# Two-layer decoder in one kernel: layer 1's attention in even rounds, transposes for selections, 23 expert slots

## The chip, the cores and the metric

The kernel runs on one core of a Trainium2 chip. The metric is device time in microseconds (us) of the whole kernel, median of several runs. TensorE, VectorE, ScalarE, GpSimd and SyncE are called PE, DVE, ACT, POOL and SP as in the profile; PEld is TensorE's loading of stationary operands.

## The reference, cut to what matters

The input is x, 8 sequences of 256 tokens by 128 features (2048 tokens, 16 tiles of 128), and a context of 8 x 256 x 256. All is float32. Six blocks follow each other, each added to x, each on a layer norm of x:

```python
x = x + _L0_attn_ref(_layernorm(x), ...)          # gated linear attention, 8 heads, chunks of 64
x = x + _L0_xattn_ref(ctx_2048, _layernorm(x), ...)   # attention over the context, 8 heads of 16
x = x + _L0_ffn_ref(_layernorm(x), ...)           # top 1 of 8 experts, silu(a) * g @ w2
x = x + _L1_attn_ref(_layernorm(x), ...)          # latent attention, 16 heads of 8 + 4 rotated, causal
x = x + _L1_xattn_ref(ctx_2048, _layernorm(x), ...)   # attention over the context, 8 heads of 16
x = x + _L1_ffn_ref(_layernorm(x), ...)           # top 1 of 8 experts, relu, b1, b2

# _L1_attn_ref, its core
Q = concat([Qc, rope(Qr)]); K = concat([Kc, rope(Kr)])      # 12 of 32 rows used per head
scores = clip(Q @ K.T, -80, 80); scores = where(causal, scores, -inf)
attn = softmax(scores / sqrt(12)) @ V; return attn @ W_O
# _L1_xattn_ref, its core
logits = (query * 16 ** -0.5) @ K.T + b[0] + -1e30 * (1 - mask); out = softmax(logits) @ V
```

## The kernel before, in words

The 16 tiles of tokens are worked on in four quads of four tiles, that is two sequences (batches) each. In time the kernel has five stages: layer 0's attention over all quads; the sort of tokens to expert slots; layer 0's experts, which write to the DRAM tensor x_mid; layer 1's attention (causal, then context); sort and experts again, which write the output. The change is almost wholly in the fourth stage.

Every engine's instructions are written by generators, one for each quad and part (`pe_mla` and `pe_xattn` for PE, `dve_mla`, `act_mla` and so on). Each generator yields the time at which its next piece should stand, and `alternate` merges the pieces of all generators by these numbers. So a table of numbers fixes the order of each engine's queue; what really starts when is decided by semaphores. In layer 1 a quad has the period `L1_PERIOD`, 72 planned units.

A head takes a strip of 32 rows of PE's array; four heads fill it. The work of a quad in layer 1:

- **In-work.** Layer norm, four transposes of tokens (`pe_ln`, L283, by way of the helper), the latent product (L1196), the rotated queries (L1199), four products for the keys (L1202, 512 columns each), values (L1207), and for each group g of four heads the queries in two accumulating products: the plain part (L1222) and `sel_rope`, which puts the rotated part `tq` in place (L1223).
- **Causal units.** 16 units of two heads and one batch. A unit is four score products (L1242, rows 32-strip by 256 or 128 columns) into one of two pairs of PSUM banks; then DVE clips and masks (L1398, 768 columns, writes `am`), ACT takes the exponential (L1340), and PE multiplies with the values, two units in one group (L1259), into bank 7; ACT copies that (L1328).
- **Out-work.** For each batch eight products with `m_sel` (L1268) sum up and turn to tokens, DVE divides, two transposes, two products with W_O, and DVE adds to x.
- **Context units.** They belong to the quad before. For each batch four units "M" (L826, scores, then DVE's maximum L1075 over 1024 columns), a turn of the maxima to rows ("N", L852, ACT copy, DMA into a row of the queries), four units "E" (L839, scores the other way round, ACT's exponential L1004), value products (L874), and "T", four products with `x_sel` to tokens (L884). Except in the last quad they all use one pair of PSUM banks (`use_bank` gives 2).
- **Router.** Layer norm, four transposes, logits (L970), `pe_rank`, and some 30 small DVE instructions that place the tokens.

A unit of two heads takes strips 0 and 1 or strips 2 and 3. `warm` (L278) issues products that nobody reads. In the trace a product shows as two records and a transpose as one, so "L826 x8" is one unit of four products.

The experts run in `TURNS = SLOTS // 4 = 6` turns of four slots of 128 rows: `hidden(s)` (L1538), `rows_out(s)` (L1548), DVE's sum (L1647), and POOL's indirect DMA (L1455).

Of the kernel before, what the change touches and what calls it, by code (L numbers as in the profile page):

```python
# [44 lines left out]
SLOTS = 24  # L45
COL_PROB, COL_ID, ROW = 2 * D, 2 * D + 1, 2 * D + 2
# [6 lines left out]
X_COLS, M_COLS = D + XH, D + MH  # L53
# [3 lines left out]
L0_PERIOD, L1_PERIOD = 57.0, 72.0  # L57
# [3 lines left out]
def alternate(*programs):  # L61

    waiting = [[next(p), k, p] for k, p in enumerate(programs)]
    while waiting:
        first = min(waiting, key=lambda w: w[:2])
        try:
# [9 lines left out]
              ("block_mask", 128), ("reset", 512), ("x_sel", XG * X_COLS), ("iota8", 8),  # L76
# [4 lines left out]
              ("clip_mask", 3 * 128), ("lat_rope", 256), ("q_rope", 256), ("m_sel", MG * M_COLS), ("sel_rope", MG * 128)]  # L81
# [3 lines left out]
               ("r0_w", EXP), ("r0_b", EXP), ("m_lat", 128), ("m_qr", 128), ("m_q", MG * 128),  # L85
# [17 lines left out]
def build(nc, A):  # L103
    ctx = ExitStack()
    with ctx:
# [48 lines left out]
        gla_own = sb("gla_own", [P, 2 * QN])  # L154
# [71 lines left out]
        kept = sb("kept", [P, 2, 4, 2 + D])  # L226

# [21 lines left out]
        def dve_ln_stats(v, s, n, q):  # L249
            for j in range(QT):  # L250
                v.bn_stats(stats[s][:, j, :], x_all[:, q * QT + j, :]).then_inc(S(s + "_stats"), 1)
            v.wait_ge(S(s + "_stats"), (n + 1) * QT)
# [1726 lines left out]
```

## Time and profile before

| what | us |
|---|---|
| median of 3 runs (880.88, 880.92, 897.6) | 880.92 |
| the profiled execution | 885.41 |
| its span, first to last instruction | 883.1 |
| layer 1's attention in it, x_mid in SBUF to layer 1's last logits | 364.8 (434.6 to 799.4) |
| PE busy, DVE busy, ACT busy | 714.6, 426.4, 265.8 |
| mean granted clock of PE | 0.894 |

The profiled execution lies 2.3 above its span and 4.5 above the median. Busy time of PE contains waiting inside the pipeline and grows when the clock is lower, so it says little alone.

### The profile page before, as it was taken

The page shows a single profiled execution, that of the slowest core. Times are in us where ns is not written, and L with a number is a line of the kernel's source. Part 1 is how long each engine was busy: PE and PEld are TensorE (multiplying, and loading weights), DVE is VectorE, ACT ScalarE, POOL GpSimd, SP SyncE. Part 2 cuts the span into 40 slices and gives each one's busy share as a digit, 9 for nine tenths or more (in the row PEclk, how much of TensorE's full clock was granted, in tenths as well). Part 3 has the DMA queues.
Part 4 walks back from the last instruction along what each step waited for, and adds up shares of the span by engine and source line. Part 5 has one row for each costly group of instructions (what it writes and reads, how often), then busy time and mean ns, then how long its engine had stood idle before and what let it go on. Part 6 is the DMA issues. An engine that isn't in the chain of part 4 may idle for free.

```text
span 883.1 us, 13749 instructions
## 1 busy us (share of the span) xinstructions
PE 714.6 (81%) x5218; PEld 475.4 (54%) x5219; DVE 426.4 (48%) x1130; ACT 265.8 (30%) x457; POOL 141.2 (16%) x163
## 2 busy tenths in 40 slices
PE   4788988888988863899698888898889888863885
PEld 2353554554555442899446455555464556432775
DVE  1556466756736425233245553555446644533453
ACT  1323323422430220222135135213522352130331
POOL 3221021211211102133200100100110011021333
PEclk9988999999998786999789997988699879885998
DMA  9600000000002004677310000100010001002762
GB/s 351 258 26 0 2 1 25 25 2 25 6 21 97 35 38 142 193 229 235 107 66 32 1 1 2 49 0 2 25 49 1 2 25 50 1 25 66 206 182 71
DMA packets 37798, 59.07 MB, mean 67 GB/s; under 512 B 9520, under 2 KB 26032, under 8 KB 36848
## 3 DMA queue, kind: packets, MB, share of 16 engines
q1 hardware_dynamic: 34384, 46.76, 17.1%
q0 software_dynamic: 3072, 7.38, 2.3%
q10 hardware_dynamic: 288, 4.19, 1.3%
q8 instruction: 36, 0.59, 0.3%
q14 instruction: 18, 0.15, 0.1%
HBM read 50.68 MB, written 13.71 MB: 73 GB/s over the span
## 4 chain that ended last, share of the span: by engine, by line
PE 67%; DVE 11%; ACT 9%; issue 5%; DMA 5%; POOL 2%; SPq 1%; POOLq 0%; ACTq 0%; DVEq 0%
PE ps L1538 7%; PE ps L826 7%; PE ps L278 6%; PE ps L839 6%; PE ps L874 4%; PE ps L1548 4%; PE ps L1242 3%; DVE neg_max L1075 3%; PE ps L1259 2%; ACT pT L1004 2%; PE ps L884 2%; PE ps L1222 2%; PE ps L1268 2%; PE ps L1202 2%; PE ps L896 2%
## 5 line engine op out<-in xcount | busy, mean ns | idle before, releaser
L1075 DVE TENSOR_REDUCE neg_max<-ps 128x4 f32<-128x1024 f32 x64 | 78.2, 1225 | 77.9 <-PE ps L826 77.8
L278 PE MATMUL ps<-cst 128*128 128x512 f32 (+1 forms) x126 | 74.5, 725 | 36.4 <-DMA sorted<-rows_all,pos 24.6
L1398 DVE SCALAR_TENSOR_TENSOR am<-ps,cst 128x768 f32<-128x768 f32 x64 | 60.2, 953 | 45.8 <-PE ps L1242 45.8
L1538 PE MATMUL ps<-pT,w 128*128 128x128 f32 x576 | 72.6, 280 | 10.7 <-issue 5.6
L1340 ACT ACTIVATE w<-am 128x768 f32<-128x768 f32 x64 | 53.9, 842 | 81.1 <-DVE am L1398 72.4
L1538 PEld LDWEIGHTS ps<-pT,w 128*128 128x128 f32 x576 | 67.9, 194 | 14.0 <-issue 10.0
L1440 POOL DMA_INDIRECT sorted<-rows_all,pos x32 | 32.7, 1021 | 189.4 <-DVE pos L393 182.1
L1242 PE MATMUL ps<-qa,ka 32*128 32x128 f32 (+1 forms) x512 | 61.3, 375 | 0.3 <-DVE am L1398 0.3
L278 PEld LDWEIGHTS ps<-cst 128*128 128x128 f32 x126 | 26.6, 233 | 64.3 <-issue 56.1
L1242 PEld LDWEIGHTS ps<-qa,ka 32*128 32x128 f32 x512 | 48.4, 208 | 15.7 <-issue 9.1
L839 PE MATMUL ps<-qs,gla_own 32*128 32x256 f32 x256 | 44.6, 493 | 10.0 <-ACT pT L1004 8.3
L826 PE MATMUL ps<-gla_own,qs 32*128 32x256 f32 x256 | 40.3, 436 | 12.1 <-ACT pT L1004 7.4
L1002 ACT ACTIVATE pT<-ps 128x1024 f32<-128x1024 f32 x32 | 32.4, 1024 | 54.6 <-PE ps L839 54.1
L1004 ACT ACTIVATE pT<-ps,wts 128x1024 f32<-128x1024 f32 x32 | 35.5, 1112 | 28.8 <-PE ps L839 28.7
L826 PE MATMUL ps<-ka,qs 32*128 32x256 f32 x256 | 33.7, 411 | 9.5 <-DVE qs L1059 5.0
L271 POOL TENSOR_TENSOR ve_x<-mv_x,cst 128x4 f32<-128x4 f32 x16 | 4.1, 254 | 231.2 <-DVE mv_x L255 231.2
L826 PEld LDWEIGHTS ps<-gla_own,qs 32*128 32x128 f32 x256 | 23.8, 200 | 26.7 <-DVE neg_max L1075 8.8
L839 PEld LDWEIGHTS ps<-qs,gla_own 32*128 32x128 f32 x256 | 27.3, 239 | 19.2 <-ACT pT L1004 11.8
L1091 DVE RECIPROCAL rden<-ps 128x16 f32<-128x16 f32 x16 | 4.1, 257 | 68.0 <-PE ps L884 68.0
L839 PE MATMUL ps<-qs,ka 32*128 32x256 f32 x256 | 34.1, 428 | 3.0 <-DMA qs<-nm_rows 2.7
L1259 PE MATMUL ps<-w,vm 128*32 128x128 f32 (+1 forms) x512 | 33.7, 379 | 1.7 <-ACT w L1328 0.5
L721 POOL TENSOR_TENSOR qe_bd<-gla_own,cst 128x512 f32<-128x512 f32 x16 | 17.0, 1073 | 105.9 <-DVE gla_own L633 58.1
(249 smaller groups left out, 1268.1 us busy)
## 6 DMA issues: line engine op xcount, KB each, us to landing
w<-in_w SPq DMA_DIRECT2D x24, 512.0 KB, 3.6
sorted<-in_no_rows SPq DMA_DIRECT2D x2, 3096.0 KB, 23.2
w<-in_w SPq DMA_DIRECT2D x24, 256.0 KB, 3.0
w<-in_w ACTq DMA_DIRECT2D x2, 2048.0 KB, 8.7
pT<-sorted SPq DMA_DIRECT2D x12, 256.0 KB
kept<-sorted SPq DMA_DIRECT2D x12, 256.0 KB
ctxT<-in_ctxT SPq DMA_DIRECT2D x4, 512.0 KB, 4.2
gla_own<-in_keys SPq DMA_DIRECT2D x4, 512.0 KB, 4.4
```

Source lines behind the costliest of these rows:

```text
L278: pe.matmul(bank(b)[:, 0:cols], ident, cst[:, 0:cols], start=True, stop=True)
L826: i = pe.matmul(bank(use_bank(layer, "M", e, q) + jj)[:, qt * T:(qt + 1) * T], qs[r, g, q0:q0 + P], kl[r, g, b * T:(b + 1) * T], start=Tru ...
L839: i = pe.matmul(bank(use_bank(layer, "E", e, q) + jj)[:, kt * T:(kt + 1) * T], kl[r, g, k0:k0 + P], qs[r, g, b * T:(b + 1) * T], start=Tru ...
L874: i = pe.matmul(bank(V_BANK[layer], STRIP, STRIP * k)[:, g * T:(g + 1) * T], xv[layer][:, 2 * b + kt, h0 + k, :], p, start=(kt == 0), stop ...
L1004: i = a.activation(out, scores, ACT.Exp, bias=W("x1_b"))
L1075: v.tensor_reduce(neg_max[:, 2 * b:2 * b + 2, h0:h0 + 2].rearrange("p t j -> p j t"), ps[:, p:p + 2, :].rearrange("p j (t k) -> p j t k", ...
L1242: i = pe.matmul(bank(M_PAIRS[u % 2][jj])[:, to], ka[r:r + STRIP, g, b * T + lo:b * T + lo + P], qa[r:r + STRIP, g, b * T + lo:(b + 1) * T] ...
L1259: i = pe.matmul(o, vm[:, 2 * b + kt, 2 * hp + k, :], p, start=(kt == 0), stop=(kt == 1), skip_group_check=True)
L1340: a.activation(view[0], view[1], ACT.Exp, scale=float(MD + MR) ** -0.5).then_inc(S("mp"), 1)
L1398: v.scalar_tensor_tensor(out[:, :, 0:3 * P], ps[:, 4 * (u % 2):4 * (u % 2) + 2, 0:3 * P], -CLIP, C("clip_mask").unsqueeze(1).broadcast_to( ...
L1538: k = pe.matmul(bank(lane(s) + 1 + half)[:, at * P:(at + 1) * P], w1[:, s * cols + c * P:s * cols + (c + 1) * P], xsT[:, s, :], start=True ...
L1548: k = pe.matmul(bank(lane(s))[:, 0:D], hidT[s][:, j * P:(j + 1) * P], wsrc[:, bass.ds(es[s] * (4 * D) + j * D, D)], start=(j == 0), stop=( ...
```

## The change

Layer 0's attention keeps its order; only its "T" step becomes four transposes with the identity instead of four products with `x_sel` (136 columns), and DVE picks the heads out of the strips. Layer 1's attention is rewritten:

- The unit of time is a **round**, one causal unit n = 0 to 63, over all four quads without a break. Context units stand at fixed rounds: for batch h M at 8h + 13, 14, 17, 18 and E ten rounds later, so from round 13 on a round has at most one. By these numbers the context unit takes strips 0 and 1 when the causal unit takes 2 and 3, and the other way round. It stands ahead of the causal unit on PE.
- From unit 12 on all causal units use the pair of banks 0 and 1 (`m_pair`), and the context units banks 2 and 3, until the causal ones are done; then they take turns on both pairs. All other work shares banks 4 and 5 in turn (`SHARED`, `wait_for_shared`).
- In-work of a quad is spread over rounds 4.7 to 16.6 of the quad before, out-work over the rounds after. Keys, values and some queries have a second buffer (`m_keys`, `m_values`, `qa_odd`).
- Queries: two products `m_qa` and `m_qb` of the latent, DVE multiplies by the rotation, multiplies the other half and adds (three instructions in place of one); then one product for each four heads in place of two.
- `m_sel` is gone: eight transposes for a batch instead of eight products of 144 columns; DVE divides tile by tile.
- Layer 1's context keys come in 8 pieces into three buffers, its values in 8 pieces.
- `keep_busy` puts a product that nobody reads (256 columns) ahead of each context unit after round 65.
- POOL sets `mask_row` (128 x 2048) to 1 after the first experts.
- 23 slots (`USED`) are worked instead of 24: the last turn of each expert stage has three.

The core of the diff:

```diff
+USED = B * T // P + EXP - 1
-L0_PERIOD, L1_PERIOD = 57.0, 72.0
+L0_PERIOD = 57.0
...
+        MU = MH // 2
+        MX = QB * MU
+        X_LAG = 13
+        def xm_at(h, i):
+            return MU * h + X_LAG + i // 2 * 4 + i % 2
+        def xe_at(h, i):
+            return MU * h + X_LAG + 10 + i // 2 * 4 + i % 2
+        IN_AT = {"ln": 4.70, "lat": 5.70, "qa": 6.20, "qb": 6.70, "k": (7.30, 7.70, 8.30, 14.10), "v": 10.80,
+                 "q": (13.60, 14.85, 15.20, 16.60)}
+        IN_AT_0 = dict(IN_AT, k=(7.20, 17.15, 17.60, 19.40), v=15.60, q=(7.70, 16.70, 17.90, 20.60))
+        OUT_AT = {"tok": (9.45, 9.70), "turn": 10.05, "out": 10.55, "strips": 11.40, "N": X_LAG + 7.85, "T": X_LAG + 18.60}
+        R_AT = {"L": X_LAG + 28.90, "R": X_LAG + 29.40, "rank": X_LAG + 31.40}
+        def shared(*use):
+            return 4 + SHARED.index(use) % 2
+        def m_pair(n):
+            return 2 if n < X_LAG - 1 and n % 2 else 0
...
-                pe.matmul(o, W("m_q")[:, g * P:(g + 1) * P], lat, start=True, stop=False)
-                pe.matmul(o, C("sel_rope")[:, g * P:(g + 1) * P], tq, start=False, stop=True)\
-                  .then_inc(S("mq_ps"), 1)
+                    pe.matmul(bank(shared(*use)), W("m_q")[:, g * P:(g + 1) * P], tq, start=True, stop=True)\
+                      .then_inc(S("mq_ps"), 1)
...
+            for n in range(MX * q, MX * (q + 1)):
+                yield n + 0.05
+                scores(n)
+                if n % MX >= 2 and n % 2 == 0:
+                    yield n + 0.60
+                    values(n - 2)
...
-                        i = pe.matmul(bank(b)[:, t * M_COLS:(t + 1) * M_COLS],
-                                      m_on[b][g // 2][:, g % 2 * T + t * P:g % 2 * T + (t + 1) * P],
-                                      C("m_sel")[:, g * M_COLS:(g + 1) * M_COLS], start=(g == 0),
-                                      stop=(g == MG - 1))
+                    i = pe.transpose(bank(shared("tok", h, t))[:, g * P:(g + 1) * P],
+                                     m_on[b][g // 2][:, g % 2 * T + t * P:g % 2 * T + (t + 1) * P], ident)
...
-                        i = pe.matmul(bank(use_bank(layer, "T", b, q))[:, t * X_COLS:(t + 1) * X_COLS],
-                                      on[b][:, g * T + t * P:g * T + (t + 1) * P],
-                                      C("x_sel")[:, g * X_COLS:(g + 1) * X_COLS], start=(g == 0), stop=(g == XG - 1))
+                        i = pe.transpose(bank(use_bank("T", b))[:, (t * XG + g) * P:(t * XG + g + 1) * P],
+                                         on[b][:, g * T + t * P:g * T + (t + 1) * P], ident)
...
+        def keep_busy(pe, at):
+            if at >= MX * QUADS + 1:
+                pe.wait_ge(S("mo"), MG * QUADS)
+                warm(pe, 7, 1, T)
...
+            v.tensor_tensor(tri3(tq, QB), tri3(bank(shared("qa", q)), QB), rope("qa_rope"), ALU.mult)\
+             .then_inc(S("tq"), 1)
...
+            v.tensor_tensor(tri3(tq_sin, QB), tri3(bank(shared("qb", q), 64, 64), QB),
+                            C("qb_rope", 64, 64).unsqueeze(1).broadcast_to([64, QB, T]), ALU.mult)\
+             .then_inc(S("tq"), 1)
+            v.wait_ge(S("tq"), 3 * q + 2)
+            v.tensor_tensor(tq[64:P, :], tq[64:P, :], tq_sin, ALU.add).then_inc(S("tq"), 1)
...
+            g.wait_ge(S("mask1"), 5)
+            g.memset(mask_row[:, :], 1.0).then_inc(S("cleared"), 1)
...
-                hidden(3)
+                if not last:
+                    hidden(3)
```

PE in the middle of layer 1's attention, before: causal units (L1242) of the second quad with context units (L839, L826) between them. Not every causal unit has one ahead, and there is no other work in this stretch.

```order
L1242 MATMUL ps<-qa,ka 128x256 [waits ms_read,mqa]
L1242 MATMUL ps<-qa,ka 128x256
L1242 MATMUL ps<-qa,ka 128x128 x2
L839 MATMUL ps<-qs,gla_own 128x256 [waits mx_read]
L839 MATMUL ps<-qs,gla_own 128x256 x3
L1242 MATMUL ps<-qa,ka 128x256 [waits ms_read]
L1242 MATMUL ps<-qa,ka 128x256
L1242 MATMUL ps<-qa,ka 128x128 x2
L826 MATMUL ps<-gla_own,qs 128x256 [waits ex_read]
L826 MATMUL ps<-gla_own,qs 128x256 x3
```

The same engine and stage after the change, rounds 27 and 28: E units are L1388, causal scores L1292, causal values L1308; L1352 are the transposes of the next context queries, L1414 the maxima of a batch.

```order
L1388 MATMUL ps<-qs,gla_own 128x256 [waits mx_read]
L1388 MATMUL ps<-qs,gla_own 128x256 x3
L1292 MATMUL ps<-kept,w 128x256 [waits ms_read]
...
L1352 MATMUL ps<-cst,xn_pad 128x128 [waits x_xn,x_attn]
L1352 MATMUL ps<-cst,xn_pad 128x128
...
L1388 MATMUL ps<-qs,gla_own 128x256 [waits ex_read]
L1388 MATMUL ps<-qs,gla_own 128x256 x3
L1292 MATMUL ps<-qa,w 128x256 [waits ms_read]
...
L1308 MATMUL ps<-w,mask_row 32x256 [waits mp]
...
L1414 MATMUL ps<-cst,neg_max 8x128 [waits nm_b,mva]
```

What moved: every round now has one context unit ahead of one causal unit, and the full-width work of the quad stands between them.

PE at the start of layer 1's attention, before: L1196 latent, L1199 rotated queries, L1202 all four keys, L1207 values, L1222 and L1223 queries, L1242 the first causal unit.

```order
L1196 MATMUL ps<-xnT_a,wts 128x512 [waits a_xnT]
L1199 MATMUL ps<-gate,wts 128x512 [waits lat]
L1202 MATMUL ps<-gate,wts 128x512 x4
L1207 MATMUL ps<-wts,gate 128x128 [waits tq]
L1207 MATMUL ps<-wts,gate 128x128 x3
L1222 MATMUL ps<-gate,wts 128x512 [waits mka]
L1223 MATMUL ps<-w,cst 128x512
L1222 MATMUL ps<-gate,wts 128x512 [waits mka]
L1223 MATMUL ps<-w,cst 128x512
L1242 MATMUL ps<-qa,ka 128x256 [waits mqa,mka]
```

The same place after: L1253 latent, L1259 the two products for the queries, L1266 one group of keys, L1275 one group of queries, L1270 values, L1292 the first causal unit.

```order
L1253 MATMUL ps<-xnT_a,wts 128x512 [waits a_xnT]
L1259 MATMUL ps<-ctxT,wts 128x512 [waits lat,a_xnT]
L1259 MATMUL ps<-ctxT,wts 128x512 [waits lat]
L1266 MATMUL ps<-ctxT,wts 128x512 [waits tq]
L1275 MATMUL ps<-ctxT,wts 128x512 [waits tq]
L1270 MATMUL ps<-wts,ctxT 128x128 [waits mka]
L1270 MATMUL ps<-wts,ctxT 128x128 x3
L1292 MATMUL ps<-qa,ka 128x256 [waits mqa,mka]
```

What moved: three of four key products and the second group of queries now stand behind the first causal unit.

## Rows read from the trace of the kernel before

**Rows 1.** The page: busy time (share of the span) of each engine

```profile
PE 714.6 (81%) x5218; PEld 475.4 (54%) x5219; DVE 426.4 (48%) x1130; ACT 265.8 (30%) x457; POOL 141.2 (16%) x163
```

**Rows 2.** Windows of layer 1's attention: stretch, busy time by engine, PEclk

```profile
core 0: us, PE busy (x) PEld busy (x) DVE busy (x) ACT busy (x) POOL busy (x), PEclk, DMA share, GB/s
434.60:453.90 19.30, 17.75 (x36) 7.67 (x36) 4.44 (x16) 3.58 (x6) 1.24 (x2) 0.66 0.27 85
453.90:491.00 37.10, 31.51 (x319) 20.50 (x318) 22.47 (x47) 16.63 (x23) 1.51 (x4) 1.00 0.16 58
...
591.40:641.50 50.10, 43.73 (x382) 26.47 (x380) 25.84 (x52) 21.96 (x27) 3.93 (x4) 0.76 0.03 12
641.50:678.50 37.00, 33.28 (x208) 20.76 (x206) 20.29 (x68) 8.84 (x15) 3.70 (x6) 0.95 0.10 30
...
751.80:786.80 35.00, 28.94 (x206) 16.81 (x206) 15.51 (x43) 9.03 (x10) 3.92 (x4) 0.80 0.05 17
786.80:799.40 12.60, 7.04 (x40) 4.49 (x40) 3.68 (x18) 2.31 (x3) 1.24 (x2) 0.85 0.00 0
```

**Rows 3.** Timeline of PE in the rounds of quad 1: start, us, operation

```profile
601.14 1.13 PE L1222 MATMUL ps<-gate,wts 128*128 128x512 f32 x2
602.11 1.02 PE L1223 MATMUL ps<-w,cst 128*128 128x512 f32 x2
603.06 1.13 PE L826 MATMUL ps<-gla_own,qs 32*128 32x256 f32 x8
604.03 0.82 PE L1242 MATMUL ps<-qa,ka 32*128 32x256 f32 x8
...
608.32 0.48 PE L826 MATMUL ps<-gla_own,qs 32*128 32x256 f32 x2 [0.97 <-ACT pT L1004]
608.35 0.48 PE L1242 MATMUL ps<-qa,ka 32*128 32x256 f32 x2
...
609.07 0.38 PE L826 MATMUL ps<-gla_own,qs 32*128 32x256 f32 x2
609.38 0.86 PE L1259 MATMUL ps<-w,vm 128*32 128x256 f32 x16
```

**Rows 4.** Timeline of PE: eight transposes, context values, four products of 136 columns

```profile
667.22 1.04 PE L923 MATMUL ps<-cst,xn_pad 128*128 128x128 f32 x8
...
783.52 1.07 PE L874 MATMUL ps<-pT,qe_bd 128*32 128x256 f32 x16 [1.34 <-ACT pT L1004]
784.52 1.19 PE L884 MATMUL ps<-cst,on 128*128 128x136 f32 x8
```

**Rows 5.** Groups of DVE, 434 to 797 us: busy us, mean ns, idle before

```profile
L1398 DVE SCALAR_TENSOR_TENSOR am<-ps,cst 128x768 f32<-128x768 f32 x64 | 60.2, 953 | 45.8 <-PE ps L1242 45.8
L1075 DVE TENSOR_REDUCE neg_max<-ps 128x4 f32<-128x1024 f32 x32 | 39.2, 1226 | 44.2 <-PE ps L826 44.2
...
L1364 DVE TENSOR_TENSOR gate<-ps,cst 128x512 f32<-128x512 f32 x4 | 2.8, 692 | 4.9 <-PE ps L1196 4.7
```

**Rows 6.** Timeline of PE at the start of layer 1's attention

```profile
434.62 3.75 PE L278 MATMUL ps<-cst 128*128 128x512 f32 x4 [6.56 <-DMA rows_all<-x_mid]
...
444.70 5.03 PE L1202 MATMUL ps<-gate,wts 128*128 128x512 f32 x8
...
453.99 0.92 PE L1242 MATMUL ps<-qa,ka 32*128 32x256 f32 x8
```

**Rows 7.** Windows of 1 us around a fall of the clock

```profile
613.00:614.00 1.00, 0.00 (x0) 0.00 (x0) 0.00 (x0) 1.00 (x3) 0.00 (x0) 1.00 0.00 0
614.00:615.00 1.00, 0.93 (x8) 0.68 (x8) 0.00 (x0) 0.75 (x2) 0.00 (x0) 0.91 0.00 0
615.00:616.00 1.00, 1.00 (x12) 0.40 (x12) 0.52 (x1) 0.00 (x0) 0.00 (x0) 0.50 0.06 16
```

**Rows 8.** Timeline of POOL, last turn of layer 1's experts, first and last of four

```profile
871.04 0.96 POOL L1455 DMA_INDIRECT out_x<-pT,kept  x1 [3.14 <-DVE pT L1647]
...
875.34 0.95 POOL L1455 DMA_INDIRECT out_x<-pT,kept  x1 [0.30 <-issue]
```

More of the change, by code:

```diff
@@ new lines, in build, with x1_event @@
+        STRIPS_LN, ROUTER_LN = 10.97, X_LAG + 27.00
+        X_LNS = sorted([(MU * h + STRIPS_LN, "x", h) for h in range(BATCHES)]
+                       + [(MX * q + ROUTER_LN, "r", q) for q in range(QUADS)])
+        def x1_event(own, k):
+            at = [e[1:] for e in X_LNS].index((own, k))
+            ahead = sum(2 if e[1] == "x" else QT for e in X_LNS[0:at])
+            size = 2 if own == "x" else QT
+            return 2 * QUADS + at, 2 * QUADS * QT + ahead, range(k * size, (k + 1) * size)
@@ new lines, in x_unit_at, with x_pair, wait_for_pair @@
+        def x_unit_at(kind, h, i):
+            return X_UNITS.index(((xm_at if kind == "M" else xe_at)(h, i), kind, h, i))
+        def x_pair(kind, h, i):
+            return X_PAIRS[x_unit_at(kind, h, i)]
+        def wait_for_pair(pe, kind, h, i):
+            at = x_unit_at(kind, h, i)
+            same = [k for k in range(at) if X_PAIRS[k] == X_PAIRS[at]]
+            if not same:
+                pe.wait_ge(S("ms_read"), X_LAG - 1 if X_PAIRS[at] == 2 else MX * QUADS)
+                return
+            _, kind, h, i = X_UNITS[same[-1]]
+            pe.wait_ge(S("mx_read" if kind == "M" else "ex_read"), X0 + UB * h + i + 1)
@@ L1239, in scores @@
+        def pe_mla(pe, q):
+            keys = m_keys[q % 2]
+            def scores(n):
+                if n % MX in (0, 2, 4, 6):
+                    pe.wait_ge(S("mka"), MG * q + n % MX // 2 + 1)
+                    pe.wait_ge(S("mqa"), MG * q + n % MX // 2 + 1)
+                same = [k for k in range(n) if m_pair(k) == m_pair(n)]
+                if same:
+                    pe.wait_ge(S("ms_read"), same[-1] + 1)
                 for lo, to in ((0, slice(0, T)), (P, slice(T, T + P))):
@@ new lines, in pe_router @@
+        def pe_router(pe, q):
+            yield shared_at("L", q)
+            wait_for_shared(pe, "L", q)
+            if q == QUADS - 1:
+                warm(pe, shared("L", q), 2)
+            pe_ln(pe, "x", x1_event("r", q), shared("L", q))
+            yield shared_at("R", q)
+            wait_for_shared(pe, "R", q)
+            pe.wait_ge(S("x_xnT"), 2 * QUADS + q + 1)
+            logits(pe, 1, shared("R", q))
+            if q < QUADS - 1:
+                yield shared_at("rank", q)
+                wait_for_shared(pe, "rank", q)
+                pe_rank(pe, QUADS + q, q, bank(shared("rank", q))[:, 0:R_COLS])
@@ L1564, in turn @@
                 rows_out(2)
-                rows_out(3)
+                if not last:
+                    rows_out(3)
             pe.wait_ge(S("slots"), layer + 1)
@@ L1599, in turn @@
                     hidden(pair)
-                    hidden(pair + 1)
+                    if pair == 0 or not last:
+                        hidden(pair + 1)
                     if not last:
```

1230 lines of the change are left out of this document (684 added, 546 removed), and 12 rows, old and new, of the table PLACES.

## The prediction, made before the changed kernel had run

> **What bounds the kernel now.** I read the busy times first: PE is busy for 81% of the span, DVE for 48%, ACT for 30% [rows 1]. In layer 1's attention, where the change sits, the windows say more. It lasts 364.8 us, and a quad costs 50.1 us of rounds (16 causal units, most with a context unit) and 37.0 us of in-work, out-work and the first context units, in which no causal unit runs [rows 2]. The sum, 87.1 us, comes three times. In the rounds PE is busy for 43.7 of 50.1 us but at a mean clock of 0.76; since it has two levels, 1.2 and 2.4 GHz, that is 48% of the time at the lower one. DVE is busy for 25.8 + 20.3 = 46.1 us of the 87.1 [rows 2]. So PE sets the time, partly by its low clock, partly because causal units and the other work of a quad don't overlap.
>
> The timeline shows the second reserve. A context unit and a causal unit on the same strips go one behind the other: L826 from 603.06, L1242 from 604.03 to 604.85, 1.79 us. On opposite strips they run together: both start at 608.32 and 608.35 and the last ends at 609.45, 1.13 us [rows 3].
>
> **The steady rounds (13 to 63).** PE's work for one quad, that is 16 rounds, at the full clock:
> - 16 pairs of units on opposite strips at 1.13: 18.1 us [rows 3].
> - 8 groups of causal values at 0.86: 6.9 [rows 3]. 4 groups of context values at 1.07: 4.3 [rows 4].
> - In-work: latent, 2 for the queries, 4 keys, 4 queries are 11 full products (before 14: 1 + 1 + 4 + 8); two of them take 603.06 - 601.14 = 1.92, so 0.96 each [rows 3]. With the values, about one more: 12 x 0.96 = 11.5.
> - 44 transposes (16 tokens, 4 turned, 8 strips, 8 context tokens, 8 layer norm) at 1.04 / 8 = 0.13: 5.7. 14 small products (W_O, maxima, logits, rank) at 1.19 / 4 = 0.30: 4.2 [rows 4].
>
> The sum is 50.7 us, 3.17 for a round. These durations hold the tail of each group, so a change from strips to full width is in them.
>
> DVE's work does not shrink: 46.1 us for a quad, plus two instructions of 0.69 for the queries' rotation, is 47.5 us, 2.97 for a round [rows 2, 5]. Most of it is the mask, 0.953 for each unit, and the maximum, 1.226 for each M unit [rows 5]. The two engines are nearly level, and from unit 12 on the causal scores have one pair of banks: scores wait for the mask of the unit before (1.1 for the pair, 0.95 for the mask, and in M rounds 1.23 for the maximum ahead of it on DVE, 3.3 if nothing overlapped). What PE does in DVE's time are values and shared work. On PE, behind each wait for `ms_read` stands everything else in its queue, so a late mask holds back in-work as well. I take the share that PE reached in the rounds before, 43.7 / 50.1 = 87% [rows 2]: 3.17 / 0.87 = 3.64, and 3.7 with a little of the low clock. The floor is 3.2 (PE never waits); the upper bound 4.6, if a wait of about 1 us like those for ACT (0.97 at 608.32, [rows 3]) is added to each round. 51 rounds x 3.7 = 189 us.
>
> **The ends of the stage.** Lead-in: before, 454.0 - 434.6 = 19.4 us [rows 6]. Three key products (5.03 / 4 = 1.26 each), one group of queries (1.9) and the second product of the other (1.0) leave it, 6.7 us; one product (1.0 to 1.9 by the clock) and two DVE instructions of 0.69 come in, 2.9 [rows 3, 5, 6]. 19.4 - 3.8 = 15.6. Rounds 0 to 12: alone the 16 causal units took 37.1 us, 2.3 each [rows 2]. Some 14 full products (13.4 us) and about 20 transposes and small products (3) are spread over 13 rounds, beside 13 x (0.82 + 0.43) = 16 us of units [rows 3, 4]; 33 us of PE work against a chain of 30 gives 2.7 a round, 35 us. After round 63 there are 17 context units; before, 16 took 35.0 us [rows 2], so 37, and 2 for the last out-work: 39. The end, last E unit to last logits, was 12.6 [rows 2] and loses 0.6 in its transposes: 12.
>
> Sum: 15.6 + 35 + 189 + 39 + 12 = 290.6 us against 364.8, a gain of 74.2.
>
> **The rest.** Layer 0's "T": four products cost 1.19, four transposes 4 x 0.13 = 0.52 [rows 4]; 8 x 0.67 = 5.4 if all of it were on the path, nothing if other work hid it. PE is the chain there, so I take 3.5. The 24th slot: POOL's scatters start 871.04 to 875.34, (875.34 - 871.04) / 3 = 1.4 each [rows 8], and PE loses one `hidden` and one `rows_out` ahead of them; 1.4 to 2.8 a stage, I take 2, twice 2 = 4. POOL's memset of `mask_row` runs while x_mid is on its way (PE waits 6.56 us for it, [rows 6]), so it costs nothing; if it slipped behind the first layer norm it would cost some 2 us. The extra DMAs of keys are prefetched several rounds ahead and cost nothing unless SP's queue, in which they stand ahead of the maxima's rows, is held by an `ex_ps` wait; then one E unit is late.
>
> Total gain 74.2 + 3.5 + 4 = 81.7. The profiled execution would go from 885.4 to 803.7. It lay 4.5 us above the median of the runs, so I forecast **799 us**.
>
> **A rule against it.** The transposes take the place of products that also kept the clock up. What this trace shows is only that the clock falls after a wait: PE idle from 613 to 614, full clock until 614.8, half at 615, with PE busy again [rows 7]. Among the rounds after, 5.7 of 50.7 us are transposes. The Trainium skill, "TensorE: Matmul & The Clock Gate", part 4, says that transposes don't count as busy for the clock. No row here separates that. By the rows alone the sum stays at 799; by the page the rounds would have 11% more idle time for the clock, and the sum would move towards the 843 of the second rival.
>
> **The rivals.**
> - *Denser.* Tuned tables hide more and PE waits little: 3.3 a round, 51 x 0.4 = 20 us less, 779. For it: PE's demand is spread over all rounds. Against: in-order queues on three engines with only two shared banks. 12%.
> - *The clock stays as bad.* At half clock PE's work doubles: two dummy products took 3.75 at the start, 1.87 each, against 0.96 [rows 3, 6], x 1.95. A fully slow stage would be: 51 x 3.17 x 1.95 = 315 instead of 189 (taking no waits), early rounds 33 x 1.95 = 64 instead of 35, the tail some 20 more: 175 in all. In the six windows shown the slow share was 2 x (6.6 + 0 + 12.0 + 1.9 + 7.0 + 1.9) of 191 us, 31% [rows 2]; I have 6% in the forecast. The same 31% costs 0.25 x 175 = 44: 843. For it: the waits for ACT and DVE that made it fall. Against: in the 16 rounds with causal units alone, with PE waiting for DVE in each, the clock was 1.00 throughout [rows 2]. 14%.
> - *The clock turns it over, slower than before.* If each round holds a wait long enough, PE stays low. The gain of 82 is gone at 82 / 175 + 0.06 = 53% of the stage at the lower level, and 2% (17.6 us) is lost at 63%. The rounds of quad 1 already had 48% [rows 2]. A stage at 70% gives 799 + 0.64 x 175 = 911. 4%; between 850 and 898 another 4%.
> - *The pairs don't run together.* Wrong strips or the waits (causal scores wait for the mask, while the context unit already runs) put units one after the other: 0.66 us more a round if PE is the bound, 51 x 0.66 = 34: 833. For it: with single banks the context unit's bank comes free before the mask is done, so many pairs will overlap only in part, though then DVE works meanwhile. 9%, partly in the upper bound of the round already.
>
> The forecast keeps 57%.
>
> **How the numbers follow.** The floor of the rounds gives 799 - 51 x 0.5 = 773, with a few us from the ends 768; the upper bound, 4.6 a round, gives 799 + 46 = 845, which takes in the two middle rivals. 768 to 846 leaves out about 2 in 10. A measurement of this kernel tells 2%, 17.6 us, from no change. Faster than 863: forecast, denser, both middle rivals and part of the rest, 91%. Same: 5%. Slower than 898: 4%.
>
> **What would show it.** Right: layer 1's attention near 290 us; causal scores in every round without the 37 us holes; E or M records with the causal ones inside 1.2 us; DVE busy for over 75% in the steady rounds; clock above 0.93 there; three scatters in the last turn. Wrong: rounds of over 4.5 us, PE waiting for `am` by more than 1 us in each (DVE's order is the bound), a mean clock near 0.75, or waits on shared banks 4 and 5 at the head of PE's queue. The step I trust least is the 87% that turns 3.17 into 3.64.

## The result, and the profile after

| | before | after |
|---|---|---|
| median | 886.27 us (880.88 to 897.6, 4 runs) | 796.5 us (794.86 to 801.96, 4 runs) |
| the profiled execution, its span | 885.41, 883.1 | 796.71, 794.9 |
| mean granted clock of PE | 0.894 | 0.912 |

The ratio is 0.902, with an interval of 0.892 to 0.911: faster by 10%. It leaves out the 897.6 of the kernel before, a slow run over 1.5% above its fastest. The forecast was 799.

On the page the busy time of PE falls with the span and its share hardly moves; DVE does the same work in less time [rows 1]:

```profile
PE 650.2 (82%) x5010; PEld 422.9 (53%) x5011; DVE 427.7 (54%) x1152; ACT 263.3 (33%) x454; POOL 143.5 (18%) x170
```

The windows show where. They cut layer 1's attention into the parts of the forecast: lead-in, rounds 0 to 12, rounds 13 to 63, tail to the last E unit, and the end (the last logits end at 712.56). They answer to [rows 2].

```profile
core 0: us, PE busy (x) PEld busy (x) DVE busy (x) ACT busy (x) POOL busy (x), PEclk, DMA share, GB/s
427.86:443.49 15.63, 13.69 (x27) 5.67 (x27) 5.80 (x18) 1.20 (x2) 1.24 (x2) 0.59 0.39 119
443.49:479.30 35.81, 32.97 (x255) 18.79 (x254) 22.55 (x46) 16.92 (x25) 2.10 (x4) 0.98 0.16 60
479.30:649.00 169.70, 155.03 (x1607) 94.78 (x1604) 129.27 (x307) 85.48 (x119) 14.32 (x24) 0.96 0.07 20
649.00:699.30 50.30, 43.71 (x318) 25.45 (x318) 24.17 (x88) 16.27 (x20) 9.97 (x12) 0.93 0.08 28
699.30:712.56 13.26, 8.99 (x36) 4.85 (x36) 3.47 (x16) 2.31 (x3) 1.24 (x2) 0.66 0.00 0
```

The stage takes 712.6 - 427.9 = 284.7 us where it took 364.8: 80.1 of the 88.2 us by which the span shrank. The other 8.1: x_mid is in SBUF 6.7 us earlier, and what follows the last logits takes 82.3 in place of 83.7.

A steady round lasts 169.7 / 51 = 3.33 us. PE is busy for 91% of it and DVE for 76%, at a clock of 0.96; the rounds of quad 1 had 0.76 before. In the timeline of PE below, an M unit and a causal unit on opposite strips start 0.03 us apart and the last ends 1.14 us after the first start, as the one pair in [rows 3] did.

```profile
559.74 0.48 PE L1376 MATMUL ps<-gla_own,qs 32*128 32x256 f32 x2
559.77 0.48 PE L1292 MATMUL ps<-qa,ka 32*128 32x256 f32 x2
...
560.31 0.39 PE L1292 MATMUL ps<-qa,ka 32*128 32x128 f32 x4
560.50 0.38 PE L1376 MATMUL ps<-gla_own,qs 32*128 32x256 f32 x2
```

DVE's groups on the page answer to [rows 5]. The mask costs 950 ns as before, but the idle time ahead of it is 11.2 us where it was 45.8: the stretches without causal units are gone. Ahead of the maximum it is 30.7 where it was 44.2.

```profile
L1550 DVE SCALAR_TENSOR_TENSOR am<-ps,cst 128x768 f32<-128x768 f32 x64 | 60.8, 950 | 11.2 <-PE ps L1292 10.6
...
L1590 DVE TENSOR_REDUCE neg_max<-ps 128x4 f32<-128x1024 f32 x32 | 39.2, 1224 | 30.7 <-PE ps L1376 30.7
```

In the waits of PE from 479.3 to 649, the largest is for DVE's layer norm, not for the mask, and all recorded waits together are 14.3 us of 170:

```profile
engine line waited for: us in total, times, longest us
PE ps L1352 <- DVE xn_pad L286: 5.9, 6, 1.4
...
PE ps L1376 <- DVE neg_max L1590: 1.5, 5, 0.4
...
PE ps L1292 <- DVE am L1550: 0.7, 2, 0.5
```

The timeline of all engines around one M unit (line L1376, round of 546.63) shows a chain over two engines:

```profile
546.63 0.48 PE L1376 MATMUL ps<-gla_own,qs 32*128 32x256 f32 x2
546.66 0.48 PE L1292 MATMUL ps<-qa,ka 32*128 32x256 f32 x2
...
547.82 1.23 DVE L1590 TENSOR_REDUCE neg_max<-ps 128x4 f32<-128x1024 f32 x1 [1.17 <-PE ps L1376]
...
548.28 1.07 PE L1402 MATMUL ps<-pT,qe_bd 128*32 128x256 f32 x16
548.96 0.95 DVE L1550 SCALAR_TENSOR_TENSOR am<-ps,cst 128x768 f32<-128x768 f32 x1
...
549.56 0.38 PE L1329 MATMUL ps<-cst,gate 128*128 128x128 f32 x2
...
549.87 0.48 PE L1376 MATMUL ps<-gla_own,qs 32*128 32x256 f32 x2
550.05 0.48 PE L1292 MATMUL ps<-qa,ka 32*128 32x256 f32 x2
```

The pair takes 1.2 us, then come the maximum and behind it the mask, which ends at 549.91. The next pair starts 3.24 us after the last: its context unit at 549.87 behind PE's transposes, its causal unit at 550.05 behind the mask. So PE's queue and the chain over DVE end almost together here, and these rows alone don't tell which sets the pace. The experiments do.

The last turn of layer 1's experts has three scatters, 1.27 us apart [rows 8]:

```profile
784.73 0.96 POOL L1698 DMA_INDIRECT out_x<-pT,kept  x1 [3.67 <-DVE pT L1900]
...
787.26 0.96 POOL L1698 DMA_INDIRECT out_x<-pT,kept  x1 [0.30 <-issue]
```

### The profile page after: what moved, and what is told of

The parts are those of the page before. It is cut to its first block, busy times and chain, and to the rows that moved or that the text cites. A ratio compares the mean times of both kernels' runs of the same rounds, so it can differ in the third digit from the quotient of the medians.

```text
span 794.9 us, 13449 instructions
## 1 busy us (share of the span) xinstructions
PE 650.2 (82%) x5010; PEld 422.9 (53%) x5011; DVE 427.7 (54%) x1152; ACT 263.3 (33%) x454; POOL 143.5 (18%) x170
## 4 chain that ended last, share of the span: by engine, by line
PE 65%; DVE 15%; ACT 7%; issue 6%; DMA 3%; POOL 3%; SPq 0%; POOLq 0%; ACTq 0%; DVEq 0%
PE ps L1788 8%; PE ps L302 6%; PE ps L1798 5%; PE ps L1376 3%; PE ps L1388 3%; PE ps L843 3%; PE ps L830 3%; PE ps L1292 3%; PE ps L1308 2%; PE ps L872 2%; PE ps L892 2%; DVE neg_max L1063 2%; DVE am L1550 2%; PE ps L308 2%; PE ps L1275 2%
## 5 line engine op out<-in xcount | busy, mean ns | idle before, releaser
L302 PE MATMUL ps<-cst 128*128 128x512 f32 (+1 forms) x110 | 64.1, 710 | 34.4 <-DMA sorted<-rows_all,pos 23.8
L1788 PE MATMUL ps<-pT,w 128*128 128x128 f32 x552 | 69.2, 279 | 11.6 <-issue 4.8
L1788 PEld LDWEIGHTS ps<-pT,w 128*128 128x128 f32 x552 | 64.2, 192 | 15.6 <-issue 11.1
L1550 DVE SCALAR_TENSOR_TENSOR am<-ps,cst 128x768 f32<-128x768 f32 x64 | 60.8, 950 | 11.2 <-PE ps L1292 10.6
L1590 DVE TENSOR_REDUCE neg_max<-ps 128x4 f32<-128x1024 f32 x32 | 39.2, 1224 | 30.7 <-PE ps L1376 30.7
L302 PEld LDWEIGHTS ps<-cst 128*128 128x128 f32 x110 | 23.4, 239 | 57.8 <-issue 51.1
L984 ACT ACTIVATE pT<-ps 128x1024 f32<-128x1024 f32 x32 | 32.4, 1024 | 54.4 <-PE ps L843 49.4
L293 POOL TENSOR_TENSOR ve_x<-mv_x,cst 128x4 f32<-128x4 f32 (+1 forms) x16 | 4.1, 253 | 250.1 <-DVE mv_x L273 250.1
L1376 PE MATMUL ps<-gla_own,qs 32*128 32x256 f32 x256 | 38.1, 417 | 2.1 <-DVE neg_max L1590 1.5
L1388 PE MATMUL ps<-qs,gla_own 32*128 32x256 f32 x256 | 37.3, 409 | 2.9 <-ACT pT L1500 1.4
L830 PEld LDWEIGHTS ps<-ka,qs 32*128 32x128 f32 x256 | 21.9, 194 | 21.1 <-issue 11.6
L1698 POOL DMA_INDIRECT x_mid<-pT,kept x23 | 22.0, 959 | 59.1 <-DVE pT L1900 55.4
L1388 PEld LDWEIGHTS ps<-qs,gla_own 32*128 32x128 f32 x256 | 22.5, 189 | 15.0 <-issue 9.5
L1376 PEld LDWEIGHTS ps<-gla_own,qs 32*128 32x128 f32 x256 | 23.0, 194 | 13.6 <-issue 6.3
```

The source lines that it names most:

```text
L302: pe.matmul(bank(b)[:, 0:cols], ident, cst[:, 0:cols], start=True, stop=True)
L830: i = pe.matmul(bank(use_bank("M", e) + jj)[:, qt * T:(qt + 1) * T], qs[r, g, q0:q0 + P], kl[r, g, b * T:(b + 1) * T], start=True, stop=True)
L1376: k = pe.matmul(bank(x_pair("M", h, i) + jj)[:, qt * T:(qt + 1) * T], qs[r, g, cols + qt * P:cols + (qt + 1) * P], kl[r, g, :], start=True ...
L1388: k = pe.matmul(bank(x_pair("E", h, i) + jj)[:, kt * T:(kt + 1) * T], kl[r, g, kt * P:(kt + 1) * P], qs[r, g, cols:cols + T], start=True, ...
L1550: v.scalar_tensor_tensor(out[:, :, 0:3 * P], ps[:, m_pair(n):m_pair(n) + 2, 0:3 * P], -CLIP, C("clip_mask").unsqueeze(1).broadcast_to([P, ...
L1590: v.tensor_reduce(neg_max[:, t, 2 * i:2 * i + 2].rearrange("p t j -> p j t"), ps[:, p:p + 2, :].rearrange("p j (t k) -> p j t k", t=2), AX ...
```

## The experiments

All are edits of the changed kernel. I read them by stretches, because one stretch without any edit differs between executions: the tail from the last causal scores to the last E unit (start to start) took from 47.3 to 68.6 us, in step with its clock (below). For rounds 13 to 63 (first M unit to last causal scores) the changed kernel has 169.4; the four executions that follow whose instructions there are the same had 169.3, 169.6, 167.6 and 166.0. Their mean is 168.4. They go with the clock: 169.6 at 0.94; 169.4, 169.3 and 167.6 at 0.96; 166.0 at 0.98. An edit that moves the clock in these rounds is therefore mispriced by the mean alone.

So each edit is also read where the clock is the same. From the start of the mask of round 21 to that of round 53 it was 1.00 in these five executions and in most of the edited ones. In these 32 rounds (16 with an M unit, 16 with an E unit; called **the clean stretch** below) the five take 106.3 to 106.5 us, 3.33 a round. Of the changed kernel:

```profile
510.39:616.88 106.49, 99.21 (x1074) 58.88 (x1074) 83.03 (x191) 58.86 (x80) 10.00 (x16) 1.00 0.08 24
```

**1. Does the overlap on opposite strips carry the gain?**

```diff
-            return n // MU % QB, hp // 2, STRIP * (2 * (hp % 2) + jj)
+            return n // MU % QB, hp // 2, STRIP * (2 * (1 - hp % 2) + jj)
...
-                        p = pTm[:, (n + k // 2) % 3, k % 2 * 512 + lo:k % 2 * 512 + to]
+                        p = pTm[:, (n + 1 - k // 2) % 3, k % 2 * 512 + lo:k % 2 * 512 + to]
```

> The changed kernel with the causal units of each batch in the other order of their two pairs of heads, so that from round 13 on a causal unit has the same strips as the context unit beside it; no work is added. Theory A, the overlap on opposite strips carries the gain and TensorE is the bound: 51 rounds x 0.66 us = 34 us more, 830. Theory B, TensorE waits in each round for the mask anyway and the overlap is worth little: under 10 us more.

Runs of 812.3, 836.1, 836.8 and 839.7 us. Of the profiled one (839.7), the rounds and the tail:

```profile
482.70:674.20 191.50, 183.98 (x1606) 122.00 (x1602) 132.00 (x307) 84.53 (x118) 14.28 (x24) 0.93 0.06 18
674.20:741.30 67.10, 61.95 (x322) 34.50 (x320) 24.29 (x88) 16.56 (x21) 9.95 (x12) 0.64 0.06 21
```

The rounds cost 23 us more, 0.45 each, at a clock of 0.93 in place of 0.96. In rounds 29 to 53, at 1.00 here as without the edit, it is 91.6 us in place of 80.6: 0.46 each. The tail is another 17 us longer at a clock of 0.64, though its instructions are the same; so the total of 840 is no measure of the overlap. Theory A has the right cause and too high a price: a pair that doesn't overlap costs 0.66 more on PE, and about two thirds of that arrives. That the rest falls into time in which PE waited before fits, but is not shown. Theory B is out.

**2. Which engine sets the rounds?** One edit puts a product of 256 columns ahead of the causal scores, another a maximum of 384 columns ahead of the mask:

```diff
+                warm(pe, m_pair(n), 1, T)
                 for lo, to in ((0, slice(0, T)), (P, slice(T, T + P))):
```

```diff
+                v.tensor_reduce(extra[:, n:n + 1], ps[:, m_pair(n), 0:3 * P], AX.X, ALU.max)
                 out = cl[:, n % 2, :].rearrange("p (a c) -> p a c", a=2)
```

> The changed kernel with one more product that nobody reads (256 columns, full width, 0.5 to 0.6 us) ahead of the scores of each of the 64 causal units. Theory A, TensorE is the bound in the rounds: 0.5 x 64 = 32 us more. Theory B, VectorE's order is the bound: TensorE has 0.3 us of idle time in a round and more that is waiting within busy time, so under 12 us more.

> The changed kernel with one more maximum over 384 columns of the scores on VectorE ahead of the mask of each of the 64 causal units (0.5 us each; its result is not used). Theory A, TensorE is the bound: VectorE has 0.8 us of idle time a round and takes it up, under 10 us more. Theory B, VectorE is the bound or its mask is in the chain of every round: 0.5 x 64 = 32 us more.

The medians are 853.9 and 827.0 us. Rounds 13 to 63, of the first and of the second:

```profile
484.50:699.80 215.30, 211.53 (x1708) 126.95 (x1704) 135.30 (x307) 86.37 (x119) 14.33 (x24) 1.00 0.06 16
```

```profile
481.20:664.40 183.20, 165.84 (x1604) 103.45 (x1602) 152.18 (x358) 85.21 (x118) 14.28 (x24) 0.93 0.07 19
```

The product costs 46.9 us, 0.92 each, though its clock is better. In the clean stretch it takes 144.8 us in place of 106.4: 1.20 each, twice the 0.6 that it lasts. The maximum (550 ns, x51, 28 us) costs 14.8, 0.29 each, but at a lower clock; in rounds 21 to 45, at 1.00 in both, it is 84.7 in place of 80.0 us, 0.20 each, about a third of its length. In rounds 0 to 12 the two cost 3.3 and 1.0 us in all. So theory B of the first is out, and its theory A has the bound right but the price of one product at less than half. Of the second neither theory holds: DVE's extra work is in part taken up and in part in the chain. The rest of the second one's 30 us is mostly its tail, 62.7 us at a clock of 0.73.

**3. Why so much for a product of 0.6?** It stood between the context unit and the causal unit. The same product ahead of both, for both kinds of context unit, then for M alone and for E alone:

```diff
                 wait_for_pair(pe, "M", h, i)
+                if xm_at(h, i) < MX * QUADS:
+                    warm(pe, x_pair("M", h, i), 1, T)
...
                 wait_for_pair(pe, "E", h, i)
+                if xe_at(h, i) < MX * QUADS:
+                    warm(pe, x_pair("E", h, i), 1, T)
```

> The changed kernel with the same extra product of 256 columns, now ahead of the context unit in place of between the context unit and the causal unit: 48 of them, in rounds 13 to 63. Between the two it cost 45.9 us over 51 rounds, 0.90 each, more than its own 0.60. Theory A, a full-width product between two units of strips also ends their overlap: ahead of both it costs its own 0.5 to 0.6, so 24 to 29 us in the rounds. Theory B, the place doesn't matter and each costs 0.9: 43 us in the rounds.

> The changed kernel with the extra product of 256 columns ahead of the 26 M units in rounds 13 to 63 alone. With both kinds it cost 11.0 us in these rounds, 0.23 each. Theory A, there are two kinds of rounds: with an M unit the chain pair of units (1.2), VectorE's maximum (1.23), mask (0.95) sets the length and TensorE's other work has room; with an E unit, or none, TensorE's own queue sets it. Then these 26 cost under 3 us in the rounds. Theory B, all rounds are alike: 26 x 0.23 = 6 us.

> The same with the product ahead of the 21 E units in rounds 13 to 63 alone. Theory A: TensorE's queue sets these rounds, so 0.4 to 0.5 each, 8 to 11 us in the rounds. Theory B, all rounds alike: 21 x 0.23 = 5 us.

The first expectation miscounts: it is 26 + 21 = 47 products. Medians 820.0, 809.8 and 805.1 us. The rounds with both kinds, with M, and with E:

```profile
479.10:659.50 180.40, 167.37 (x1693) 99.20 (x1694) 130.26 (x307) 84.78 (x118) 14.27 (x24) 1.00 0.07 19
```

```profile
479.90:658.70 178.80, 163.79 (x1651) 97.65 (x1652) 129.75 (x307) 84.82 (x118) 14.28 (x24) 0.97 0.07 19
```

```profile
479.60:651.50 171.90, 158.70 (x1646) 95.83 (x1644) 129.53 (x307) 85.52 (x118) 14.28 (x24) 0.99 0.07 20
```

Ahead of both it costs 12.0 us, 0.26 each, against 0.92 between them; in the clean stretch 119.5 us, 0.41 each, against 1.20. The place decides, as theory A of the first has it. The timeline shows why, between the two and ahead of both:

```profile
564.18 1.13 PE L1389 MATMUL ps<-qs,gla_own 32*128 32x256 f32 x8
565.24 0.70 PE L302 MATMUL ps<-cst 128*128 128x256 f32 x2
565.87 0.92 PE L1293 MATMUL ps<-qa,ka 32*128 32x256 f32 x8
```

```profile
562.95 0.70 PE L302 MATMUL ps<-cst 128*128 128x256 f32 x2
563.58 0.48 PE L1378 MATMUL ps<-gla_own,qs 32*128 32x256 f32 x2
563.61 0.48 PE L1292 MATMUL ps<-qa,ka 32*128 32x256 f32 x2
```

Between the two it splits the pair. 0.6 for the product and 0.66 for the lost overlap make 1.3, close to the 1.20.

Over all the rounds the other two cost 10.4 us for the 26 ahead of M (0.40 each) and 3.5 for the 21 ahead of E (0.17), which looks like two kinds of rounds. But their clocks differ, 0.97 and 0.99. In the clean stretch they take 113.7 and 112.5 us, 0.46 for each of 16 M units and 0.38 for each of 16 E units. So theory A (M rounds have room on PE) is out, and theory B, all rounds alike, is nearly right, at a higher price than its 0.23. Each product lengthens its own kind of round (M from 3.52 to 3.99, E from 3.14 to 3.55) and the other hardly.

**4. Is the maximum in the chain?**

```diff
-  ps[:, p:p + 2, :].rearrange("p j (t k) -> p j t k", t=2), AX.X, ALU.max,
+  ps[:, p:p + 2, :].rearrange("p j (t k) -> p j t k", t=2)[:, :, :, 0:T:2], AX.X, ALU.max,
```

> The changed kernel with VectorE's maximum of an M unit over every second key, 512 of 1024 columns; it leaves out the other half of the maximum. The instruction should take 0.7 us in place of 1.23. Theory A, the chain over the maximum and the mask sets the M rounds: up to 26 x 0.55 = 14 us less in rounds 13 to 63, at least 7. Theory B, TensorE sets all rounds: under 2 us less.

The instruction takes 692 ns. The rounds of the profiled execution:

```profile
479.40:640.00 160.60, 148.91 (x1606) 91.30 (x1602) 116.97 (x307) 85.04 (x118) 14.28 (x24) 0.98 0.07 22
```

7.8 us less than the mean, but 5.4 less than the execution without the edit that also had 0.98. In the clean stretch:

```profile
506.38:610.62 104.24, 98.02 (x1075) 57.65 (x1074) 75.73 (x191) 58.65 (x80) 9.98 (x16) 1.00 0.08 25
```

2.2 us less, 0.14 for each of 16 units out of 0.53 saved. From mask to mask the M rounds go from 3.52 to 3.15 us, so the maximum is in their chain; the E rounds go from 3.14 to 3.37, so most of the gain is given back a round later, behind other work. At the same clock the result lies between the theories: more than nothing, less than the 7 us of theory A. The median, 794.1, hardly shows it; the tail of the profiled execution took 68.6 us at a clock of 0.63.

**5. What do transposes save?** In one kernel layer 0's T, in another 144 transposes of layer 1's attention become products with the identity; each edit has this form:

```diff
-  i = pe.transpose(bank(use_bank("T", b))[...], on[b][...], ident)
+  i = pe.matmul(bank(use_bank("T", b))[...], on[b][...], ident, start=True, stop=True)
```

> The changed kernel with layer 0's step T as 32 products with the identity in place of 32 transposes (the values are the same). Theory A, the term of the forecast: 3.5 us more, seen as a later first scatter of layer 0's experts. Theory B, other work hides the step or the spread of the clock in layer 0 is larger than it: within 1 us of the changed kernel.

> The changed kernel with 144 transposes of layer 1's attention (causal tokens, turn, strips, context tokens) as products with the identity; the values are the same. Theory A, TensorE is the bound and the clock stays as it is: 144 x 0.17 = 24 us more. Theory B, the rule that transposes don't keep the clock up decides: with products the clock is 1.00 in the rounds and above 0.9 in the tail in every execution, and the kernel is less than 12 us slower, or faster.

Layer 0: median 798.7 us over 6 runs, ratio 0.902 (0.897 to 0.906), the same as with transposes. The first scatter of layer 0's experts starts at 362.3; the executions with transposes had it at 358.3 to 366.2, the kernel before at 362.7. Theory B: nothing to be seen, within that spread.

Layer 1: median 802.6, ratio 0.908 (0.904 to 0.912). The rounds:

```profile
481.30:650.90 169.60, 158.66 (x1706) 103.13 (x1702) 130.47 (x308) 85.55 (x118) 14.28 (x24) 1.00 0.07 21
```

Some 98 more records of PE in this window, 98 x 0.17 = 17 us by the price of [rows 4], cost 1.2 us in all. That looks as if they were free, and they were not: two things hide in it. In the clean stretch:

```profile
508.64:619.93 111.29, 106.32 (x1144) 66.83 (x1142) 84.05 (x191) 58.97 (x80) 9.97 (x16) 1.00 0.08 23
```

There 68 products in place of transposes cost 4.9 us, 0.07 each. And the busy time of their groups grew by 8.5 us, 0.125 each and not 0.17 (12 us and not 17 over all rounds). So more than half of the work arrives. Outside the stretch the clock paid it back: the eight rounds ahead of it, from the mask of round 13 to that of 21, took 25.0 us at 1.00, and 26.3 to 27.8 us at 0.81 to 0.94 in the five executions with transposes.

Theory A falls in its size and in its clock. Of theory B the sizes came true (under 12 us slower; clock 1.00 in the rounds, 0.97 in the tail, though of one execution). The five executions with transposes and nothing added had 0.94 to 0.98 in the rounds; two that kept all transposes but had full-width products added had 0.99 and 1.00 (experiment 3). Adding full-width products went with a better clock as well, so this doesn't show that transposes count less for it.

**Experiments 1 to 5 at the same clock (1.00):**

| edit | us in place of | for each | its own length |
|---|---|---|---|
| product between the units of a pair | 144.8, 106.4 | 1.20 | 0.6, and 0.66 of overlap |
| pair on the same strips (24 rounds) | 91.6, 80.6 | 0.46 | 0.66 |
| product ahead of both units | 119.5, 106.4 | 0.41 | 0.6 |
| transpose as a product | 111.3, 106.4 | 0.07 | 0.125 |
| maximum ahead of the mask (24 rounds) | 84.7, 80.0 | 0.20 | 0.55 |
| half of the maximum left out | 104.2, 106.4 | -0.14 | -0.53 |

Of work on PE more than half arrives in the time, of work on DVE about a third. By these shares PE's queue is the larger part of the bound, and the chain over DVE is the rest.

**6. The 24th slot**

```diff
-USED = B * T // P + EXP - 1
+USED = SLOTS
```

together with the fourth slot of the last turn and the counts of the waits that follow from it.

> The changed kernel with 24 expert slots in both stages, four in the last turn. Theory A: first to last scatter of layer 0's experts 66.7 us in place of 64.3, of layer 1's 50.8 in place of 49.4, so 4 us more. Theory B, the last turn is bounded by something else: under 1 us more.

The source view of the scatters, with 24 slots and with 23 (the changed kernel):

```profile
L1698 POOL DMA_INDIRECT x_mid<-pT,kept x24: 956/960/962, 366.2 to 433.2; - x24
L1698 POOL DMA_INDIRECT out_x<-pT,kept x24: 956/962/1079, 738.4 to 789.0; - x24
```

```profile
L1698 POOL DMA_INDIRECT x_mid<-pT,kept x23: 953/959/962, 358.3 to 422.6; - x23
L1698 POOL DMA_INDIRECT out_x<-pT,kept x23: 955/960/1079, 737.9 to 787.3; - x23
```

67.0 against 64.3 and 50.6 against 49.4: 2.7 + 1.2 = 3.9 us, theory A. In the other executions with 23 slots the two took 63.6 to 64.4 and 48.1 to 49.6, so the sum is 3.6 to 5.9. The totals (789.4 to 813.7, median 803.5) spread too much to show it.

**7. The tail.** First without `keep_busy`, then with five products that nobody reads at places where PE waits anyway:

```diff
-            if at >= MX * QUADS + 1:
+            if at >= 10 ** 6:
```

> The changed kernel without the products that nobody reads ahead of the context units after the last causal unit (16 of them, some 0.65 us each in the timeline, all on TensorE's chain). Theory A, they are pure cost: the kernel is 10 us faster, the 50 us from the last causal unit to the last E unit become 40, the clock there stays above 0.85. Theory B, they hold the clock: without them it falls towards 0.6 in that stretch, its 35 us of other TensorE work takes some 15 us more, and the kernel is 3 to 8 us slower.

```diff
+            if h == BATCHES - 1:
+                warm(pe, 7, 1, T)
             pe.wait_ge(S("moT"), h + 1)
...
+            if h == BATCHES - 1:
+                warm(pe, 7, 2)
             for t in range(2):
                 pe.wait_ge(S("x_xn"), ahead + t + 1)
...
+                if h == BATCHES - 1 and i == 0:
+                    warm(pe, x_pair("E", h, i), 2)
                 if i == 0:
                     pe.wait_ge(S("max_in"), 16 * XG * (BATCHES + h + 1))
```

> The changed kernel without the 16 products ahead of the late context units; in their place five products that nobody reads stand where TensorE waits anyway in the tail: one of 256 columns ahead of the last batch's W_O, two of 512 ahead of its strips, two of 512 ahead of its first E unit. Theory A, the clock is lost in these waits (it fell at 660 us without the products, just behind the two waits, and at 688 us with them, behind the wait for the maxima's row): it stays above 0.9 in the tail, which takes 40 to 43 us in place of 50.2, and the kernel 8 us less. Theory B, the clock there doesn't hang on these waits: it is below 0.8, the tail takes 46 us or more, no gain.

Without `keep_busy`: median 796.4, no change. The tail is 3.2 us shorter and its clock 0.75. Both theories had a part: some 9 us of products left (each took 0.52 to 0.63), and most of that came back through the clock. Timeline and windows of this run show the fall:

```profile
657.65 0.68 PE L1343 MATMUL ps<-wts,x_oT 128*128 128x128 f32 x4 [0.57 <-ACT x_oT L1484]
...
661.31 0.95 PE L1352 MATMUL ps<-cst,xn_pad 128*128 128x128 f32 x4 [1.92 <-DVE xn_pad L286]
```

```profile
657.00:660.00 3.00, 1.83 (x13) 1.20 (x12) 2.28 (x9) 0.88 (x2) 0.20 (x1) 1.00 0.02 5
660.00:663.00 3.00, 1.69 (x8) 1.30 (x10) 0.66 (x2) 0.62 (x1) 2.49 (x3) 0.74 0.13 44
663.00:666.00 3.00, 3.00 (x14) 1.57 (x14) 0.69 (x1) 1.37 (x2) 2.13 (x3) 0.50 0.24 88
```

With the waits filled the median is 786.6 us (782.3 to 795.4), ratio 0.893 (0.884 to 0.901), and the tail of the profiled execution:

```profile
645.10:686.90 41.80, 37.47 (x302) 22.56 (x298) 24.26 (x89) 15.46 (x20) 8.04 (x10) 0.92 0.07 24
```

41.8 us in place of 50.2, with the clock at 1.00 where it fell before and low only from 672 to 680. Against the kernel without `keep_busy`, which has the five products less, it is 41.8 in place of 47.0, and against the shortest tail with `keep_busy`, 47.3 at a clock of 1.00. Theory A. It is the fastest kernel of the study. Against the changed one the ratio is about 0.893 / 0.902 = 0.99; the intervals overlap and the two did not run side by side, so 1% is likely and not settled, while the 8 us in the tail are seen in one execution, of a stretch that otherwise spread by 21.

## Why the prediction came out, step by step

| term | forecast | in the trace |
|---|---|---|
| lead-in | 15.6 | 15.6 |
| rounds 0 to 12 | 35 | 35.8 |
| rounds 13 to 63 | 189 | 169.7 |
| tail | 39 | 50.3 |
| end | 12 | 13.3 |
| stage | 290.6 | 284.7 |
| layer 0's T | gain 3.5 | not to be seen |
| 24th slot | gain 4 | 3.9 (3.6 to 5.9) |

- **What bounds the kernel, and the main gain.** Right: the 37 us holes are gone, the pairs run together in 1.14 us, the clock is 0.96, and forcing the pairs apart gives back 23 us.
- **The 87% that turned 3.17 into 3.64**, the step I trusted least, was too pessimistic: PE is busy 91%, and the round is 3.33, the number of the "denser" rival. At a clock of 1.00 it is 3.33 too, so 3.17 is 95% of it, and the 87% had been read at a clock of 0.76. The form is too simple as well. If PE's sum divided by a fixed share were the time, all work put on PE would arrive and none on DVE; at the same clock 0.41 of 0.6 and 0.07 of 0.125 arrived from PE, 0.20 of 0.55 from DVE. The M rounds (3.52) contain the chain of pair, maximum and mask, whose length of 3.3 stands in my text; the E rounds (3.14) don't.
- **The tail** was mis-sized by 11 us. I took 17 context units at their old price, 35.0 us for 16 [rows 2], and gave `keep_busy` no term, though the change section describes it: 16 products at 0.52 to 0.63 us on PE's queue, some 9 us, are most of the difference. Without it the tail was 47.0, not 39, because the clock fell. Filling the waits gave 41.8.
- **The two errors**, -19 and +11 us, cancel in part; that the total was met within 3 us is in part luck.
- **The lead-in** was met with an error inside: in this execution the products ran at half clock (two rotated queries in 3.75 us). With the clock up it was 12.9.
- **Layer 0's T** was priced as if PE's chain passed every gain on. x_mid came 6.7 us earlier, but 4.4 of that lie ahead of the first scatter, within the spread of 358 to 366 between executions, and undoing the edit changed nothing. The rest is the slot.
- **The slot** was right in sum; layer 0's is worth about 3 (2.6 to 3.4) and layer 1's 1.0 to 2.5, not 2 and 2.
- **The rivals.** "The clock stays bad" did not come true in the rounds (a clock of 0.96 is a slow share of 8%, not 31%), but it did in the tail of about half the executions. "The pairs don't run together", priced at 34 us, is worth 23 in the rounds when forced.
- **The rule against it** (the Trainium skill, "TensorE: Matmul & The Clock Gate", part 4, that transposes don't count as busy for the clock) did not decide: the rounds ran at 0.96 with all their transposes, and the sum did not move towards 843. Experiment 5 has nothing against the rule (1.00 with products, 0.94 to 0.98 with transposes) and doesn't single it out, since the products also gave PE more work.

## What to carry to other kernels

When two engines are nearly level, neither one's sum is the time: add or take away a known piece of work on each and see what share arrives. Here it was more than half on PE and about a third on DVE. Never put a full-width product between two units that should overlap (1.20 us for one of 0.6); put a product that nobody reads where the engine waits. Read a small effect in the stretch where it was made: with totals that spread by 10 to 25 us through the clock of one other stretch, four runs can't show 4 us. And compare only stretches at the same granted clock: read over rounds of unlike clock, 98 transposes turned into products seemed free (1.2 us), and M and E rounds seemed to differ (0.40 and 0.17); at the same clock neither is so.

## What the runs showed of the hardware

Where the clock is the same, executions hardly differ: the clean stretch took 106.49, 106.50, 106.31, 106.49 and 106.29 us in five executions of the same instructions.

The tail's clock differs between executions and kernels though its instructions are the same but for the edits named. Tail length and mean clock in the eleven executions that have its `keep_busy` products: 47.3 at 1.00, 50.2 at 0.93, 52.2 at 0.97 (with more products), 52.5 at 0.89, 55.0 at 0.84, 57.8 at 0.79, 60.9 and 60.8 at 0.76, 62.7 at 0.73, 67.1 at 0.64, 68.6 at 0.63. The last is that of the halved maximum; its windows show how the clock fell:

```profile
648.00:652.00 4.00, 3.44 (x23) 2.16 (x24) 2.10 (x9) 0.38 (x1) 0.00 (x0) 1.00 0.01 4
652.00:656.00 4.00, 2.52 (x18) 1.59 (x16) 1.17 (x7) 1.11 (x1) 2.80 (x4) 0.88 0.10 33
656.00:660.00 4.00, 4.00 (x18) 1.94 (x16) 0.69 (x1) 1.37 (x2) 2.01 (x3) 0.50 0.27 99
```

It fell behind the waits for the last batch's W_O and strips, and did not come back at once when PE was busy throughout: here it stayed at the lower level for over 40 us; in the kernel with the same strips it fell at 690, was back for some 4 us at 713, and was low again to the end of the stage at 755. Once slow, the same units fill PE's time almost without a gap, so the busy share no longer tells a loss. What brings the clock back earlier in one execution than in another stays open.
